# Pairs of key blocks under one VectorE pass: the positive part of a key-difference product, taken on ScalarE in front of a turn's first exponential

## The chip, the cores and the metric

One core of a Trainium2 chip runs the whole kernel. The metric is the device time of one execution in microseconds (us); the kernel before takes 1810.14 us, the median of three runs (1808.87 to 1810.49).

## What is computed

The reference is one transformer block with adaptive layer norm: attention with 16 heads of 16 dimensions over 2 sequences of 2048 tokens (32 sequence-heads in all), then a shared feed-forward network and one of eight routed experts per token. The change touches the softmax of attention:

```python
energy = jnp.einsum('nqhd,nkhd->nhqk', Q, K) / jnp.sqrt(jnp.float32(HEAD_DIM))
attn = jax.nn.softmax(energy, axis=-1)
out = jnp.einsum('nhqk,nkhd->nqhd', attn, V).reshape(N, S, EMBED)
```

The softmax subtracts each query's largest energy. The kernel finds that maximum with products of its own, one head ahead of the exponentials: it need not be exact, but it must be close, since exp overflows otherwise.

## The kernel before

**Stages.** First the projections to Q, K and V (to about 135 us, already mixed with the first head's maxima), then attention over the 32 heads (to about 1366 us), then the output projection, the shared network with the routing of tokens, and the experts. Everything is written by hand: five engine queues, semaphores, and fixed places in SBUF and PSUM. The queues are in order, so the program order of each engine is the schedule.

**Q and K as sums of bf16 parts.** `q_high` and `k_high` hold two bf16 parts of each on 64 rows, twice (rows 0 to 63 for u = 0, 64 to 127 for u = 1, which are the two halves of the queries for the maxima); `q_low` and `k_low` hold the third parts and the maxima. SyncE loads them per head from `qk_parts` in HBM (`stack`).

**Maxima of a head.** `max_product` (L1149) multiplies 128 queries by 512 keys into one PSUM bank. A head has 32 pairs m = 4t + c (query tile t of 8, key block c of 4), each with a product for u = 0 and one for u = 1: 64 products of 128x512. The products go through three banks in turn (class `Ring`); a product waits until the product three places earlier was read out. For a u = 0 product with odd m (15 of the 64) ScalarE copies the bank to `unit_sb` in `carry` (L1317), which frees the bank, and VectorE reduces the copy later (`reduce_carried`, L1277). The others VectorE reduces out of PSUM (`reduce_pair`, L1266). After a head's last pair `negate` (L1284) takes the four block maxima together, and TensorE transposes the result (`turn_maxima`, L1178).

**A turn.** Attention is a loop over heads h and 16 key tiles kt. In one turn `attend_tensor` issues, in this order:

1. `max_half`: the product (first, u = 0) of the head ahead, where first = 12 + 2(kt - 1), taken modulo 32,
2. `scores(this, 1)` (L1206): the second half of tile kt's scores, 8 matmuls of 512 columns in two row groups that run beside each other, into banks that the exponential two back must have left (`s_exp_free`),
3. `max_half`: (first, u = 1),
4. `weigh(h, kt - 1)` (L1218): probabilities times values in fp32,
5. `max_pair`: (first + 1, u = 0 and 1),
6. `scores(following, 0)`: the first half of tile kt + 1.

A turn's first exponential reads item 6 of the turn before; the second reads item 2 of its own. ScalarE's turn before the change is one `carry` (of a product in item 5 of the turn before) and the two exponentials of 128x1024 (L1338). Both exponentials must be over before `weigh` of that tile. In each head one turn also has the transposed maxima (before item 4), and one has `head_copy` on ScalarE (L1344).

**After attention.** SyncE loads expert weights (`ruT` L1499, `rdT` L1501), then the rows that GpSimd scales and scatters to the experts (`sc_x`). `rgT` was loaded by GpSimd's queue during attention, one expert every third head.

## Time and profile before

| | us |
|---|---|
| runs: median (lowest, highest) | 1810.14 (1808.87, 1810.49) |
| profiled execution: span, first to last instruction | 1807.2 |
| what lies around the span, median less span | 2.9 |
| attention, per head of 16 turns (705.31 to 744.20) | 38.89 |
| TensorE busy | 1788.2 |
| VectorE busy | 1489.3 |
| ScalarE busy | 1471.9 |
| GpSimd busy | 357.0 |

The profiled execution is known by its span; the runs' times include what lies before and after it. An engine's busy time counts from an instruction's start to its end in the record. Records of one engine overlap, since an instruction can start before the end of the one ahead of it, and the ends of matmuls are modelled. The distance from one start to the next on an engine is thus the better measure of what a step costs. The granted TensorE clock is 1.0 through attention, which is the level of 2.4 GHz.

### The profile page before, as it was taken

How to read it: one execution, taken by the hardware profiler on the slowest of the kernel's cores; microseconds unless marked ns; L12 is line 12 of the kernel's file. 1: busy time of each engine (PE TensorE's matmuls, PEld its weight loads, DVE VectorE, ACT ScalarE, POOL GpSimd, SP SyncE). 2: the span in 40 equal slices, each digit the busy share in tenths (PEclk: the TensorE clock that was granted, in tenths of full speed). 3: DMA queues.
4: the chain of work that ended last, by engine and by line, in shares of the span. 5: the costliest groups of instructions: out<-in, count | busy, mean ns of one | idle time of the engine just before them, and what ended most of it. 6: DMA issues, size and time to landing. Idle time of an engine off the chain costs nothing.

```text
span 1807.2 us, 35352 instructions
## 1 busy us (share of the span) xinstructions
PE 1788.2 (99%) x13143; PEld 809.3 (45%) x13144; DVE 1489.3 (82%) x2716; ACT 1471.9 (81%) x1908; POOL 357.0 (20%) x441
## 2 busy tenths in 40 slices
PE   9999999999999999999999999999999999999997
PEld 5533333333333333333333333333326555699996
DVE  6889999999999999999999999999935422355553
ACT  6559999999999999999999999999997411254442
POOL 6655020020000000000000200001010177233333
PEclk9999999999999999999999999999999999999998
DMA  7534131232111121111313211133124733322221
GB/s 232 151 112 120 34 89 45 82 103 60 42 45 34 43 58 59 47 34 45 91 46 98 59 42 44 42 72 86 33 69 165 286 97 117 120 81 65 67 68 42
DMA packets 87294, 145.71 MB, mean 81 GB/s; under 512 B 18692, under 2 KB 53765, under 8 KB 87020
## 3 DMA queue, kind: packets, MB, share of 16 engines
q1 hardware_dynamic: 78220, 119.22, 22.2%
q0 software_dynamic: 7936, 23.10, 4.0%
q8 instruction: 92, 1.51, 0.4%
q10 hardware_dynamic: 992, 1.44, 0.2%
q14 instruction: 54, 0.44, 0.1%
HBM read 93.85 MB, written 50.36 MB: 80 GB/s over the span
## 4 chain that ended last, share of the span: by engine, by line
PE 84%; DVE 6%; DMA 5%; ACT 2%; POOL 1%; issue 1%; SPq 1%; POOLq 0%; DVEq 0%; ACTq 0%
PE ps L1218 25%; PE ps L1206 22%; PE ps L1149 14%; PE ps L1985 8%; DVE mx L1266 4%; PE ps L2008 4%; PE ps L727 3%; DMA sc_x<-n_rows 2%; DMA sorted_in<-sc_x,slot 2%; PE ps L1551 2%; PE ps L746 1%; ACT prob L1338 1%; PE ps L1521 1%; DVE mx L1277 1%; PE ps L1858 1%
## 5 line engine op out<-in xcount | busy, mean ns | idle before, releaser
L1266 DVE TENSOR_REDUCE mx<-ps 128x1 f32<-128x512 f32 x1588 | 1004.6, 684 | 11.6 <-PE ps L1149 7.4
L1338 ACT ACTIVATE prob<-ps 128x1024 f32<-128x1024 f32 x1024 | 992.8, 1021 | 3.3 <-issue 1.6
L1149 PE MATMUL ps<-k_high,q_high 64*128 64x512 bf16 x2048 | 577.5, 382 | 0.9 <-DVE mx L1266 0.2
L1218 PE MATMUL ps<-prob,vs 128*32 128x512 f32 x4096 | 545.5, 605 | 0.2 <-ACT head_out_sb L1344 0.2
L1206 PE MATMUL ps<-q_low,k_low 34*128 34x512 bf16 x2048 | 490.6, 377 | 0.0
L1206 PE MATMUL ps<-q_high,k_high 64*128 64x512 bf16 x2048 | 490.0, 376 | 0.5 <-ACT prob L1338 0.3
L1149 PEld LDWEIGHTS ps<-k_high,q_high 64*128 64x128 bf16 x2048 | 143.2, 93 | 547.1 <-DVE mx L1266 444.3
L1277 DVE TENSOR_REDUCE mx<-unit_sb 128x1 f32<-128x512 f32 x460 | 310.8, 676 | 0.0
L1317 ACT COPY unit_sb<-ps 128x512 f32<-128x512 f32 x460 | 269.6, 586 | 5.5 <-PE ps L1149 2.0
L1206 PEld LDWEIGHTS ps<-q_low,k_low 34*128 34x128 bf16 x2048 | 143.2, 94 | 118.7
L1367 POOL CAST mb<-turned_sb 16x128 bf16<-16x128 f32 x32 | 9.0, 283 | 826.4 <-ACT turned_sb L1324 814.9
L1206 PEld LDWEIGHTS ps<-q_high,k_high 64*128 64x128 bf16 x2048 | 143.6, 95 | 53.9 <-ACT prob L1338 18.9
L1218 PEld LDWEIGHTS ps<-prob,vs 128*32 128x32 f32 x4096 | 80.6, 108 | 129.5 <-issue 118.8
L1880 ACT ACTIVATE sgate<-ps 128x512 f32<-128x512 f32 x32 | 19.1, 597 | 118.3 <-PE ps L1521 118.3
L2068 DVE TENSOR_TENSOR ehT<-esig,ps 128x512 f32<-128x512 f32 x39 | 26.8, 688 | 99.4 <-PE ps L1985 99.4
L2034 ACT ACTIVATE esig<-ps 128x512 f32<-128x512 f32 x39 | 23.3, 597 | 100.6 <-PE ps L1985 100.6
L1724 DVE TENSOR_TENSOR hid<-sgate,ps 128x512 f32<-128x512 f32 x32 | 22.0, 688 | 72.2 <-ACT sgate L1880 71.8
L1985 PE MATMUL ps<-xsT,gate_w 128*128 128x128 f32 x624 | 76.6, 276 | 0.1
L1985 PEld LDWEIGHTS ps<-xsT,gate_w 128*128 128x128 f32 x624 | 74.6, 192 | 4.4 <-DVE xsT L2061 2.5
L1985 PE MATMUL ps<-xsT,up_w 128*128 128x128 f32 x624 | 76.0, 275 | 0.0
L2008 PE MATMUL ps<-rdT,ehT 128*128 x312 | 73.6, 379 | 0.0
L1985 PEld LDWEIGHTS ps<-xsT,up_w 128*128 128x128 f32 x624 | 72.8, 192 | 0.0
(173 smaller groups left out, 1445.3 us busy)
## 6 DMA issues: line engine op xcount, KB each, us to landing
k_high<-qk_parts SPq DMA_DIRECT2D x126, 128.0 KB, 2.7
qk_parts<-parts SPq DMA_DIRECT2D x32, 384.0 KB, 3.0
k_low<-qk_parts SPq DMA_DIRECT2D x128, 64.0 KB
q_high<-qk_parts SPq DMA_DIRECT2D x126, 64.0 KB, 2.4
head_out<-head_out_sb SPq DMA_DIRECT2D x31, 256.0 KB, 2.2
sorted_in<-zero_row POOLq DMA_DIRECT2D x13, 390.0 KB, 4.6
xs<-sorted_in SPq DMA_DIRECT2D x39, 130.0 KB
q_low<-qk_parts SPq DMA_DIRECT2D x128, 32.0 KB
```

What stands on the lines that cost most here:

```text
L727: mm = pe.matmul(ps[:, 2 + n % 2, :], wqkv[:, o // 2, k, (o % 2) * P:(o % 2 + 1) * P], hT[g % CPB][:, k, :], start=(k == 0), stop=(k == 1))
L1149: pe.matmul(ps[:, ring.bank((n, m, u)), :], q_high[p][mine, t * P:(t + 1) * P], k_high[p][mine, c * CH:(c + 1) * CH], start=True, stop=Tru ...
L1206: mm = pe.matmul(ps[:, bank + u, :], keys[mine, kt * P:(kt + 1) * P], queries[mine, i * CH:(i + 1) * CH], start=(low == 0), stop=(low == 1))
L1218: mm = pe.matmul(ps[32 * j:32 * j + 32, 7, :], vs[buf(h)][:, kt, :], prob[:, (kt + 1) % 2, j * CH:(j + 1) * CH], start=(kt == 0), stop=(kt ...
L1266: dve.tensor_reduce(mx[n % 2][:, at, c:c + 1], ps[:, ring.bank(what), :], AX.X, ALU.max).then_inc(s_ring, 1)
L1277: dve.tensor_reduce(mx[n % 2][:, m // CPB, m % CPB:m % CPB + 1], unit_sb[carried_before(n, m) % NCOPY][:], AX.X, ALU.max).then_inc(s_carri ...
L1317: act.copy(unit_sb[k % NCOPY][:], ps[:, ring.bank(what), :]).then_inc(s_turned, 1)
L1338: act.activation(prob[:, (kt + 1) % 2, :].rearrange("p (u c n) -> p u c n", u=2, c=2)[:, :, half, :], ps[:, bank:bank + 2, :], ACT.Exp).th ...
L1551: mm = pe.matmul(ps[:, OUT_BANK[g % 2] + t // 2, t % 2 * D:(t % 2 + 1) * D], o[:, k, t * P:(t + 1) * P], w[:, k, :], start=(k == 0), stop= ...
L1985: mm = pe.matmul(ps[:, bank, fc * P:(fc + 1) * P], w[u][:, c, fc * P:(fc + 1) * P], xsT[u][:, c, :], start=(c == 0), stop=(c == 1))
L2008: mm = pe.matmul(ps[:, 6 + u, 0:D], ehT[u][:, c, :], rdT[:, bass.ds(e, 1), c, :].squeeze(1), start=(c == 0), stop=(c == FC - 1))
L2068: dve.tensor_tensor(ehT[u][:].rearrange("p c n -> p (c n)"), esig[u][:].rearrange("p c n -> p (c n)"), ps[:, eup_bank(k), :], ALU.mult).th ...
```

## The change

Key blocks c = 2 and c = 3 of a query tile are joined for u = 0. For the unit with m mod 4 = 2 (`steps_of`), TensorE multiplies the queries not by block 2 but by the difference of the keys, block 2 less block 3 (`k_step`). ScalarE takes the positive part, Relu, into `step_sb` (`take_step`, in place of `carry`). For m mod 4 = 3 (`folded`) VectorE adds `step_sb` to the product of block 3 and takes the maximum of the sum in one `tensor_tensor_reduce`: max(q k2 - q k3, 0) + q k3 is the larger of the two. The column of block 2 in `mx` is set to the lowest value once. There are 8 such units per head, 245 in all (5 of head 1, 8 of each of heads 2 to 31); the 460 copies and the 460 reductions of copies are gone.

`take_step` stands inside `exps`, ahead of the first exponential of turn kt, and reads the product of item 1 of the same turn kt. It does so in the turns with even kt; in those with odd kt ScalarE has the two exponentials alone.

Beside it: GpSimd makes the key differences of each sequence in two bf16 parts (`key_steps`, 3 operations for each of 2 halves), SyncE stores them and loads them per head with two more transfers (`load_key_steps`); `wuT` and `wdT` are loaded later; the last expert's `rgT` is loaded after attention by SyncE, ahead of `ruT`.

```diff
-def carried(n, m, u):
-    return u == 0 and m % 2 == 1 and m != LEAD - 1 and (n >= 2 or n == 1 and m >= LEAD)
+def steps_of(n, m, u):
+    return u == 0 and m % CPB == STEP and (n >= 2 or n == 1 and m >= LEAD)
+def folded(n, m, u):
+    return u == 0 and m % CPB == STEP + 1 and steps_of(n, m - 1, u)
...
+        def key_steps(pool, step, half):
+            step(pool.tensor_tensor(k_from[half][:], k_from[half][:], k_to[half][:], ALU.subtract))
+            step(pool.tensor_copy(step_parts[half][:, 0, :], k_from[half][:]))
+            pool.tensor_tensor(step_parts[half][:, 1, :], k_from[half][:], step_parts[half][:, 0, :],
+                               ALU.subtract).then_inc(s_kstep, 1)
...
+        def load_key_steps(sp, h):
+            n = num(h)
+            sp.wait_ge(s_kstepst, 16 * HALF * (n // H + 1))
+            mine = slice(n * DH, (n + 1) * DH)
+            for part in range(2):
+                sp.dma_start(k_step[n % 2][part * LROWS:(part + 1) * LROWS, :],
+                             step_dram[part:part + 1].to_broadcast([2, B * D, CH])[:, mine, :]
+                             .rearrange("a d t -> d a t")).then_inc(s_kstep_in[n % 2], 16)
...
+            keys = k_high[p][mine, c * CH:(c + 1) * CH]
+            if steps_of(n, m, u):
+                pe.wait_ge(s_kstep_in[n % 2], 32 * (n // 2 + n % 2))
+                keys = k_step[n % 2][mine, :]
...
-                dve.tensor_reduce(mx[n % 2][:, at, c:c + 1], ps[:, ring.bank(what), :], AX.X,
-                                  ALU.max).then_inc(s_ring, 1)
...
+                if folded(*what):
+                    above = step_sb[steps_before(n, m - 1) % NSTEP][:]
+                    dve.wait_ge(s_turned, ring.taken((n, m - 1, u)))
+                    dve.tensor_tensor_reduce(above, bank, above, 1.0, LOWEST, ALU.add, ALU.max,
+                                             largest).then_inc(s_ring, 1)
+                else:
+                    dve.tensor_reduce(largest, bank, AX.X, ALU.max).then_inc(s_ring, 1)
...
-                    if m % 2 == 0:
-                        reduce_carried(dve, n, m - 1)
...
-            what, k = (who, first + 1, 0), carried_before(who, first + 1)
...
-            act.wait_ge(s_max, ring.made(what))
-            wait(act, s_carried, k - NCOPY + 1)
-            act.copy(unit_sb[k % NCOPY][:], ps[:, ring.bank(what), :]).then_inc(s_turned, 1)
+            what = (who, first, 0)
...
+            act.wait_ge(s_max, ring.made(what))
+            if k >= NSTEP:
+                act.wait_ge(s_ring, step_folded[k - NSTEP])
+            act.activation(step_sb[k % NSTEP][:], ps[:, ring.bank(what), :], ACT.Relu).then_inc(s_turned, 1)
...
                 for half in range(2):
+                    if not half and n + kt:
+                        take_step(act, n, kt)
...
-                    carry(act, KT * n + kt)
                     exps(n, kt)
...
+            sp.dma_start(rgT[:, E - 1:E], io["rgT"][:, E - 1:E]).then_inc(s_expert_late, 16)
             for e in range(E):
                 sp.dma_start(ruT[:, e:e + 1], io["ruT"][:, e:e + 1]).then_inc(s_expert_late, 16)
```

On ScalarE, in attention, before the change (`unit_sb` is a copy of a product, `prob` an exponential):

```order
L1338 ACTIVATE prob<-ps 128x2x512 [waits s_score]
L1317 COPY unit_sb_85<-ps 128x512 [waits s_carried,s_max]
L1338 ACTIVATE prob<-ps 128x2x512 [waits s_score,s_prob_free]
L1338 ACTIVATE prob<-ps 128x2x512 [waits s_score]
L1317 COPY unit_sb_84<-ps 128x512 [waits s_carried,s_max]
L1338 ACTIVATE prob<-ps 128x2x512 [waits s_score,s_prob_free]
```

The same place with the change (`step_sb` is the positive part):

```order
L1384 ACTIVATE step_sb_84<-ps 128x512 [waits s_ring,s_max,s_prob_free]
L1409 ACTIVATE prob<-ps 128x2x512 [waits s_score] x2
L1409 ACTIVATE prob<-ps 128x2x512 [waits s_score,s_prob_free]
L1409 ACTIVATE prob<-ps 128x2x512 [waits s_score]
L1384 ACTIVATE step_sb_85<-ps 128x512 [waits s_ring,s_max,s_prob_free]
```

There is now one read of a product in two turns instead of in each. On TensorE the order is that of before; with the change a turn with even kt reads (L1223 is the products of maxima, L1280 the scores, L1292 `weigh`):

```order
L1280 MATMUL ps<-q_high_94,k_high_70 128x512 [waits s_exp_free]
L1280 MATMUL ps<-q_high_94,k_high_70 128x512
L1280 MATMUL ps<-q_low_97,k_low_71 128x512 x2
L1223 MATMUL ps<-k_step_109,q_high_92 128x512 [waits s_kstep_in0,s_ring]
L1280 MATMUL ps<-q_high_94,k_high_70 128x512 [waits s_exp_free]
L1280 MATMUL ps<-q_high_94,k_high_70 128x512
L1280 MATMUL ps<-q_low_97,k_low_71 128x512 x2
L1223 MATMUL ps<-k_high_68,q_high_92 128x512 [waits s_ring]
L1292 MATMUL ps<-prob,vs_67 32x512 [waits s_exp_free]
```

The product of the difference (fourth row) stands behind the scores that the turn's first exponential reads, and that exponential now stands behind the product's reader. On VectorE, before and after around the end of a head (`mneg` is the head's negated maxima):

```order
L1266 TENSOR_REDUCE mx_80<-ps 128x1 [waits s_max] x3
L1277 TENSOR_REDUCE mx_80<-unit_sb_84 128x1 [waits s_turned]
L1266 TENSOR_REDUCE mx_80<-ps 128x1 [waits s_max] x3
L1277 TENSOR_REDUCE mx_80<-unit_sb_85 128x1 [waits s_turned]
```

```order
L1346 TENSOR_REDUCE mx_80<-ps 128x1 [waits s_max]
L1346 TENSOR_REDUCE mx_81<-ps 128x1 [waits s_max] x4
L1351 TENSOR_REDUCE mneg<-mx_80 128x16 [waits s_ring]
L1346 TENSOR_REDUCE mx_81<-ps 128x1 [waits s_max]
L1343 ISA step_sb_85,mx_81<-ps,step_sb_85 128x512 [waits s_turned,s_max]
L1343 ISA mx_81 128x1
L1346 TENSOR_REDUCE mx_81<-ps 128x1 [waits s_max] x6
```

Of eight products in two turns VectorE now reads six alone and two together; the joined pass is two rows, the pass and the write of its result.

## Rows read from the trace of the kernel before

**Rows 1.** The page: busy time by engine.

```profile
PE 1788.2 (99%) x13143; PEld 809.3 (45%) x13144; DVE 1489.3 (82%) x2716; ACT 1471.9 (81%) x1908; POOL 357.0 (20%) x441
```

**Rows 2.** Chain that ended last, 640 to 760 us, by line.

```profile
by line: PE ps L1218 40.6%; PE ps L1206 36.1%; PE ps L1149 22.9%; PE ps L1178 0.5%
```

**Rows 3.** Timeline, one steady turn: start us, us, engine line op, names, shapes, count.

```profile
712.53 0.39 PE L1149 MATMUL ps<-k_high,q_high 64*128 64x512 bf16 x2
...
712.95 0.59 ACT L1317 COPY unit_sb<-ps 128x512 f32<-128x512 f32 x1
...
713.00 1.90 DVE L1266 TENSOR_REDUCE mx<-ps 128x1 f32<-128x512 f32 x3
...
713.19 0.38 PE L1149 MATMUL ps<-k_high,q_high 64*128 64x512 bf16 x1
...
713.46 1.94 ACT L1338 ACTIVATE prob<-ps 128x1024 f32<-128x1024 f32 x2
...
713.94 1.07 PE L1218 MATMUL ps<-prob,vs 128*32 128x512 f32 x8
...
714.94 0.39 PE L1149 MATMUL ps<-k_high,q_high 64*128 64x512 bf16 x2
```

**Rows 4.** Timeline, TensorE in the last head, which has no maxima beside it.

```profile
1340.11 1.07 PE L1218 MATMUL ps<-prob,vs 128*32 128x512 f32 x8
1341.11 0.39 PE L1206 MATMUL ps<-q_high,k_high 64*128 64x512 bf16 x2
...
1342.08 0.64 PE L1218 MATMUL ps<-prob,vs 128*32 128x512 f32 x4
```

**Rows 5.** The page: groups that the change touches (busy, mean ns; idle before, releaser).

```profile
L1266 DVE TENSOR_REDUCE mx<-ps 128x1 f32<-128x512 f32 x1588 | 1004.6, 684 | 11.6 <-PE ps L1149 7.4
...
L1149 PEld LDWEIGHTS ps<-k_high,q_high 64*128 64x128 bf16 x2048 | 143.2, 93 | 547.1 <-DVE mx L1266 444.3
L1277 DVE TENSOR_REDUCE mx<-unit_sb 128x1 f32<-128x512 f32 x460 | 310.8, 676 | 0.0
```

**Rows 6.** Timeline, ScalarE: a copy out of PSUM and the exponential behind it.

```profile
1337.45 0.59 ACT L1344 COPY head_out_sb<-ps 128x512 f32<-128x512 f32 x1
1337.91 3.87 ACT L1338 ACTIVATE prob<-ps 128x1024 f32<-128x1024 f32 x4
```

**Rows 7.** Timeline, last head, where TensorE waits for an exponential.

```profile
1329.41 3.91 ACT L1338 ACTIVATE prob<-ps 128x1024 f32<-128x1024 f32 x4 [0.41 <-PE ps L1206]
...
1331.40 0.10 PEld L1206 LDWEIGHTS ps<-q_high,k_high 64*128 64x128 bf16 x2 [0.61 <-ACT prob L1338]
...
1331.94 0.16 PEld L1218 LDWEIGHTS ps<-prob,vs 128*32 128x32 f32 x8 [0.43 <-issue]
```

**Rows 8.** Timeline, the turn with the transposed maxima (L1178).

```profile
702.69 0.39 PE L1149 MATMUL ps<-k_high,q_high 64*128 64x512 bf16 x2
...
703.76 0.21 DVE L1284 TENSOR_REDUCE mneg<-mx 128x16 f32<-128x64 f32 x1
...
704.11 0.27 PE L1178 MATMUL ps<-ident,mneg 128*16 128x128 f32 x1
...
705.31 0.39 PE L1149 MATMUL ps<-k_high,q_high 64*128 64x512 bf16 x2
```

**Rows 9.** Timeline, TensorE: the pair that ends the turn of rows 3's last line.

```profile
717.46 0.39 PE L1149 MATMUL ps<-k_high,q_high 64*128 64x512 bf16 x2
```

**Rows 10.** Groups on VectorE, 1560 to 1807 us.

```profile
L2068 DVE TENSOR_TENSOR ehT<-esig,ps 128x512 f32<-128x512 f32 x39 | 26.8, 688 | 99.4 <-PE ps L1985 99.4
...
L2082 DVE CAST cix<-xs 128x1 uint32<-128x1 f32 x39 | 5.7, 147 | 0.0
```

**Rows 11.** Chain that ended last, 1412 to 1540 us, in order of time.

```profile
1422.23 15.13 DMA sc_x<-n_rows
```

**Rows 12.** Timeline, SyncE: the first eight of sixteen expert loads.

```profile
1412.73 3.85 SPq L1499 DMA_DIRECT2D ruT<-in_ruT  x8
```

**Rows 13.** Groups by line, 60 to 200 us.

```profile
L919 POOL TENSOR_TENSOR rest<-qf,parts 128x512 f32<-128x512 f32 x17 | 19.7, 1157 | 28.6 <-ACT parts L824 28.6
```

More of the change, by code:

```diff
@@ L69 @@
 SLOTS = 6
-NCOPY = 2
+NSTEP = 2
+STEP = 2
+LOWEST = -3.0e38
 BESIDE = LEAD
@@ L90, in wait, with steps_before @@
         eng.wait_ge(semaphore, n)
[L93 to L102 removed]
+def steps_of(n, m, u):
+    return u == 0 and m % CPB == STEP and (n >= 2 or n == 1 and m >= LEAD)
+def folded(n, m, u):
+    return u == 0 and m % CPB == STEP + 1 and steps_of(n, m - 1, u)
+def steps_before(n, m):
+    return sum(steps_of(k, j, 0) for k in range(n + 1) for j in range(PAIRS if k < n else m))
 class Region:
@@ L210, in block_kernel @@
         wgT = held("wgT", [P, HALF, F])
+        late_weights_at = held.at
         wuT = held("wuT", [P, HALF, F])
@@ L397, in block_kernel @@
         s_turned = sem("s_turned")
-        s_carried = sem("s_carried")
+        s_kstep = sem("s_kstep")
+        s_kstepst = sem("s_kstepst")
+        s_kstep_in = [sem(f"s_kstep_in{i}") for i in range(2)]
         s_mb = sem("s_mb")
@@ L562, in unit, with kept, full @@
             return 2 * g + o // 2 if g < CPB and o % 2 == 0 else EARLY + 2 * g + o // 2 if g < CPB else UQ * g + o
+        def kept(g, o):
+            return o >= 2 and g % CPB in (STEP, STEP + 1)
+        def full(g, o):
+            return (k_from, k_to)[g % CPB - STEP][o - 2] if kept(g, o) else qf[unit(g, o) % UQ]
+        UNITS_AT = {unit(g, o): (g, o) for g in range(NCH) for o in range(UQ)}
         def adapt(pe, first):
@@ L695, in project_sync @@
                 sp.dma_start(dst[:], src).then_inc(s_late, 16)
+            for half in range(HALF):
+                store_key_steps(sp, 0, half)
             store(CPB + 1, 2, 3)
@@ L818, in take @@
                 n = unit(g, o)
-                slot, bank, scale = n % UQ, 2 + n % 2, 0.25 if o < 2 else 1.0
+                bank, scale = 2 + n % 2, 0.25 if o < 2 else 1.0
                 act.wait_ge(s_unit, n + 1)
                 act.wait_ge(s_qf_free, n + 1)
-                act.activation(qf[slot][:], ps[:, bank, :], ACT.Identity, bias=bqk[:, o:o + 1], scale=scale)
+                if kept(g, o) and g >= CPB:
+                    act.wait_ge(s_kstepst, 16 * HALF)
+                act.activation(full(g, o)[:], ps[:, bank, :], ACT.Identity, bias=bqk[:, o:o + 1], scale=scale)
                 act.wait_ge(s_parts[n % SLOTS], 16 * (n // SLOTS + 1))
@@ L918, in remainder @@
                 pool.wait_ge(s_qbank_free, AHEAD + n + 1)
-                pool.tensor_tensor(rest[n % UQ][:], qf[n % UQ][:], parts[n % SLOTS][:, 0, :],
+                pool.tensor_tensor(rest[n % UQ][:], full(*UNITS_AT[n])[:], parts[n % SLOTS][:, 0, :],
                                    ALU.subtract).then_inc(s_rest, 1)
@@ L1077, in prepare @@
                         sp.dma_start(xg_dram[c], xg[c][:]).then_inc(s_xgst, 16)
+                if n == XB_AT + 4:
+                    for half in range(HALF):
+                        store_key_steps(sp, 1, half)
+                if n == XB_AT + 5:
+                    sp.wait_ge(s_kstepst, 16 * HALF * B)
+                    for dst, name in ((wuT, "wuT"), (wdT, "wdT")):
+                        sp.dma_start(dst[:], io[name]).then_inc(s_shared, 16)
                 if n == XB_AT + 1:
@@ L1309, in carry @@
                 first, who = first - PAIRS, n + 2
-            if g < 2 or who >= NH:
+            if kt == 0:
+                first, who = LEAD + 2 * (KT - 1) - PAIRS, n + 1
+            what = (who, first, 0)
+            if who >= NH or not steps_of(*what):
                 return
-            what, k = (who, first + 1, 0), carried_before(who, first + 1)
-            if not carried(*what):
-                return
+            k = steps_before(who, first)
             act.wait_ge(s_max, ring.made(what))
-            wait(act, s_carried, k - NCOPY + 1)
-            act.copy(unit_sb[k % NCOPY][:], ps[:, ring.bank(what), :]).then_inc(s_turned, 1)
+            if k >= NSTEP:
+                act.wait_ge(s_ring, step_folded[k - NSTEP])
+            act.activation(step_sb[k % NSTEP][:], ps[:, ring.bank(what), :], ACT.Relu).then_inc(s_turned, 1)
+        step_folded = [ring.taken((n, m + 1, 0)) for n in range(NH) for m in range(PAIRS) if steps_of(n, m, 0)]
         def take_turned(act, n):
@@ L1427, in attend_gpsimd @@
                     bias(1, 0)
+                    for half in range(HALF):
+                        key_steps(pool, step, half)
                 if n == FIRST_AT + 6:
```

67 lines of the change are left out of this document (36 added, 31 removed).

## The prediction

> **What bounds the kernel now.** I began with the page's busy shares. TensorE is busy 99% of the span [rows 1], but the ends of matmuls are modelled, so that alone proves nothing; VectorE, ScalarE and TensorE all look full in attention. The chain of waits for a stretch of attention settles it: all of it lies on TensorE, none on VectorE or ScalarE [rows 2]. Then the timeline of one steady turn [rows 3]. I measure from the pair of products that ends a turn, and call its start P = 0 (712.53). The product of item 1 of the next turn starts at 0.66, `weigh` at 1.41, the next pair at 2.41. A head is sixteen such turns.
>
> Does TensorE wait for VectorE at the end of that turn? The page puts 444.3 us of the idle time of its weight loads down to VectorE [rows 5], and that is the number on which a gain would rest. But from `weigh` to the next matmul it is 1.00 us with products of maxima behind it [rows 3], and 1.00 us in the last head, where VectorE has none left [rows 4]. So the 1.00 us is TensorE's own. The last head's turn is 1.97 [rows 4]; two more passes of 512 columns (the pair, and the two halves beside the scores, 0.22 each: the first product stands at 0.66 behind the pair and two such steps of scores) make 2.41. **TensorE is the bound, with nothing to spare, and the change takes no matmul from it.** VectorE does four products in 2.41 us and keeps up: 0.61 from start to start (1.90 less 0.68, halved) [rows 3].
>
> ScalarE has a little slack. Its two exponentials start 0.92 apart (1.94 less the 1.02 of one [rows 3]) and end at 715.40, which is 2.87; the scores that may not overwrite them start 0.66 behind the next pair, at 3.07. TensorE starts 0.05 after an exponential's end: in rows 7 the second exponential starts at 1330.33 (0.92 after the first), ends at 1331.35, and the weight load comes at 1331.40. So the slack is 3.07 - 2.87 - 0.05 = 0.15 us.
>
> **VectorE's part.** 460 reductions of copies go (310.8 us busy [rows 5]) and 245 products are no longer reduced alone, while 245 of the remaining passes become joined ones. The trace has no joined pass. Its nearest row is a 128x512 fp32 operation on an SBUF and a PSUM operand, 688 ns; the write of the result is nearest to the 128x1 operation, 147 ns [rows 10]. Start to start I take 0.70, bounds 0.61 (as a reduction) and 1.38 (the streaming of 512 elements, 688 - 147 = 541 ns, twice, and 0.15 each for overhead and write). Seven passes in two turns take 6 x 0.61 + 0.70 = 4.36 of 4.81 us. As TensorE is the bound, this gains nothing; cost 0.
>
> The Trainium skill speaks against the joined pass: "Vector Engine (DVE) Microarchitecture Reference", section "Points that are easy to get wrong", says that the scalar-tensor-tensor shape with two SBUF sources that are not bf16 runs at half throughput, since no port is left for the accumulator. Here one source is in PSUM, so by its words the rule does not bite; the trace has no accumulating operation to show it. If it did, the upper bound above would hold, and the third rival.
>
> **ScalarE's part, on which the sum rests.** Before, each turn's copy reads the pair at P: the pair ends at 0.39, the copy starts at 0.42, the first exponential at 0.93 [rows 3]. Now in a turn with even kt the positive part reads the product that starts at 0.66. That ends 0.38 later and is read 0.03 after that, so at 1.07. From the start of such a read to the exponential behind it is 0.46 where only ScalarE decides [rows 6]; I take 0.47. The exponentials then start at 1.54 and 2.46 (+0.92), the second ends at 3.48 (+1.02), and TensorE's next second-half scores can start at 3.53 (+0.05) instead of 3.07. **The exponentials came 0.61 later, 0.15 was slack, and 0.46 is lost on the engine that is the bound.** Behind these scores nothing is made up: scores to `weigh` is 0.54 alone [rows 7] plus 0.22 for the other half-product, 0.76 against the 0.75 of before (1.41 - 0.66), and 1.00 follows. So the pair after next stands at 3.53 + 0.76 + 1.00 = 5.29 instead of 4.81. From this lap 0.48, from the slack 0.46: I take **0.47 us per two turns.** The turn with odd kt cannot win it back: ScalarE has only 1.84 us of work there and stands idle, but the next positive part must wait for 5.29 + 1.07 anyhow. That is a closed loop: product, positive part, two exponentials, scores, `weigh`, pair, scores, product.
>
> How many: 245 units, of which 185 in plain turns (31 each for kt 2, 4, 6, 8, 10, 30 for kt 14), 30 at kt 12 and 30 at kt 16.
>
> - 185 x 0.47 = 87.0 us.
> - kt 12 has the transposed maxima. Before, `mneg` starts at 1.07 after one reduction, the transposition at 1.42, the next pair at 2.62 [rows 8]; with the odd turn 5.03. Now the pair's first product is not copied any more but reduced first, so `mneg` starts 0.60 later and ends at 1.88, the transposition comes at 1.93 (+0.05), 0.51 later, the next pair at 3.13. The scores after it start at 3.79, beyond 3.53, so that the loop adds nothing: 30 x 0.51 = 15.3 us.
> - kt 16: before, 2.52 (714.94 to 717.46 [rows 3, 9]) and 2.41, together 4.93; now 5.29. 30 x 0.36 = 10.8 us.
>
> Sum in attention 113.1 us.
>
> **The rest.** GpSimd's six operations on key blocks, 1.16 us each by their nearest row [rows 13], are 7 us beside a queue that idled 28.6 us in that stretch, and its results are wanted a unit later: 0, upper bound 3. If that cover were gone, ScalarE's casts would be late first. The second sequence's six, and two more loads per head on SyncE, run an entire head or more ahead of their reader: 0. `rgT` of the last expert is a seventeenth load of 512 KB ahead of `sc_x`, whose landing, 15.13 us [rows 11], waits for the sixteen and starts the chain of the scatters. They took from 1412.73 [rows 12] to 1437.36, 1.5 us each: +1.5, bounds 0 and 3.
>
> Total: +114.6. The profiled span of 1807.2 becomes 1921.8; with the 2.9 us around a span that the median has, 1924.7, as the median plus 114.6 is: **1925 us**.
>
> **The rivals.** (1) *VectorE is what bounds, and the change frees it.* For: the 444.3 us [rows 5], and VectorE's unbroken row of passes. Then two turns need 4.36 instead of 4.81, 245 x 0.45 = 110 us less: 1700 us; it decides if the positive part is not waited for and the 1.00 us shrinks. Against: the same 1.00 in the last head. If only part of this holds, it is faster by less. Chance 0.05. (2) *The product is read in time after all*, since ScalarE's exponentials have slack that I don't see; then TensorE keeps 2.41, and only kt 12 costs: between 1811 and 1827 us. Against: the order of the three queues leaves no way round it. Chance 0.04, half of it within 0.2%. (3) *The joined pass is slow* (1.38). Then VectorE, from the pair at 2.41: pass at 2.83, next 4.21, the odd turn's first product 4.82 to 5.50, and the pair after next, whose bank it holds, not before 5.55 instead of 5.29: 245 x 0.26 = 64 us more, 1989 us. It decides from a joined pass of 1.12 on. Chance 0.08. (4) *The loop holds, but loses less*, as the matmuls' modelled ends put the product's real end earlier, or the held back scores let later matmuls pack better: 0.25 to 0.4 per two turns, with kt 12 and kt 16 and the 1.5 us some 1878 to 1910. Chance 0.13. The forecast itself, 0.44 to 0.52 per two turns and the other bounds, has 0.70.
>
> **How the numbers follow.** The forecast's own range is 1916 to 1940 (185 x 0.03 below, 245 x 0.05 above, and the two small bounds). To leave out no more than 2 in 10, I reach down into the fourth case, to 1893, and up to 1945, which leaves out the third. What a measurement of this kernel can tell from no change is about 0.2%, 3.6 us. Slower by more: 0.70 + 0.13 + 0.08 and half of the second, 0.93; within it 0.02; faster 0.05.
>
> **What would show it.** Right: in turns with even kt the positive part starts about 0.03 after the end of the product beside the scores, at 1.07 behind the pair; TensorE's second-half scores of the odd turn wait for an exponential; pairs stand 2.41 and 2.88 apart in turn; ScalarE is idle before the positive part by about 1.0 us; VectorE idles in each turn; a head takes 42.5 us instead of 38.89. Wrong: pairs 2.41 apart or less throughout, no idle time of ScalarE before its read, or, for the third rival, waits of the pair for VectorE and a joined pass of over 1 us.

## The result, and the profile after

The kernel with the change takes 1942.07 us, the median of four runs (1941.20 to 1942.73), against 1810.27 beside it: **7.3% slower, ratio 1.0728 (95% interval 1.0713 to 1.0743)**. The forecast was 1925 us with a range of 1893 to 1945. The sign, the engine and the mechanism held; 132 us were lost where 114.6 were worked out. That is 2 us beyond the forecast's own bounds (1916 to 1940), and inside the stated range by 3.

The profiled execution has a span of 1939.4 us and a time of 1941.20. All of the loss is in attention: from the first to the last `weigh` it is 1366.0 us instead of 1234.2 (+131.8), the part ahead of it changed by -1.2 us (132.3 for 133.6), the part behind it by +1.7 (441.1 for 439.4).

The page, busy time by engine and the chain that ended last, by engine (the first line answers to [rows 1]):

```profile
PE 1890.8 (97%) x13143; PEld 769.3 (40%) x13144; DVE 1382.1 (71%) x2719; ACT 1352.9 (70%) x1693; POOL 367.9 (19%) x452
...
PE 56%; ACT 28%; issue 11%; DVE 4%; DMA 0%; POOLq 0%; DVEq 0%; POOL 0%; ACTq 0%
```

VectorE and ScalarE each work over 100 us less than before and the kernel is slower. TensorE is still "97% busy", although it now waits in every second turn: for a bound, this share says little. The chain does, here for 640 to 760 us (it answers to [rows 2], which held nothing but TensorE):

```profile
by line: ACT prob L1409 30.9%; PE ps L1292 21.2%; issue 16.6%; PE ps L1280 12.2%; ACT step_sb L1384 9.5%; PE ps L1223 7.0%; DVE mx L1346 2.1%; PE ps L1252 0.5%; DVE mneg L1351 0.2%
```

One lap of two turns of it, start, length and what:

```profile
743.26 1.04 PE ps L1292 x8
744.30 1.01 issue
745.32 0.60 ACT step_sb L1384
745.91 1.84 ACT prob L1409 x2
747.75 0.05 issue
747.80 0.61 PE ps L1280 x4
748.40 0.22 PE ps L1223
748.62 1.04 PE ps L1292 x8
```

That is the forecast's closed loop: 748.62 - 743.26 = 5.36 us. (The four matmuls of L1280 are one half of a tile's scores, two with `q_high` and two with `q_low`; item 2 of a turn has four, not eight.) The 1.01 us of "issue" are the pair, the scores and the difference product between `weigh` and the positive part, which the chain couldn't tie to it. The timeline shows them (start us, us, engine line op, names, shapes, count; it answers to [rows 3]):

```profile
744.19 0.39 PE L1223 MATMUL ps<-k_high,q_high 64*128 64x512 bf16 x2
...
744.85 0.38 PE L1223 MATMUL ps<-k_step,q_high 64*128 64x512 bf16 x1
...
745.32 0.60 ACT L1384 ACTIVATE step_sb<-ps 128x512 f32<-128x512 f32 x1 [1.10 <-issue]
745.36 0.09 PEld L1223 LDWEIGHTS ps<-k_high,q_high 64*128 64x128 bf16 x1 [0.19 <-DVE mx L1346]
...
745.81 3.77 ACT L1409 ACTIVATE prob<-ps 128x1024 f32<-128x1024 f32 x4
...
746.68 0.39 PE L1223 MATMUL ps<-k_high,q_high 64*128 64x512 bf16 x2
...
747.10 0.69 DVE L1343 CUSTOM_DVE_ANT_0 step_sb<-ps,step_sb 128x512 f32<-128x512 f32 x1 [0.60 <-PE ps L1223]
...
747.72 0.08 DVE L1343 DVE_READ_ACCUMULATOR2_ANT mx<- 128x1 f32 x1
747.72 1.88 DVE L1346 TENSOR_REDUCE mx<-ps 128x1 f32<-128x512 f32 x3
747.79 0.10 PEld L1280 LDWEIGHTS ps<-q_high,k_high 64*128 64x128 bf16 x2 [0.58 <-ACT prob L1409]
...
748.55 0.16 PEld L1292 LDWEIGHTS ps<-prob,vs 128*32 128x32 f32 x8 [0.43 <-issue]
```

ScalarE sits idle for 1.10 us, reads the product that it had to wait for, and its second exponential ends late enough to hold TensorE's scores for 0.58. The pair comes at 744.19 and 746.68, 2.49 apart; the next one 2.87 behind that (2.87 or 2.88 in all plain laps). VectorE idles 0.60 in front of the joined pass. TensorE's one wait for it in these rows, the 0.19 at 745.36, lies inside the lap and costs nothing here. The groups of the page say the same over the program (busy, mean ns; idle before, releaser; the second and third lines answer to the first two of [rows 5], whose third has no counterpart):

```profile
L1384 ACT ACTIVATE step_sb<-ps 128x512 f32<-128x512 f32 x245 | 146.5, 598 | 244.2 <-issue 242.1
...
L1346 DVE TENSOR_REDUCE mx<-ps 128x1 f32<-128x512 f32 x1558 | 982.2, 684 | 88.0 <-PE ps L1223 84.3
L1223 PEld LDWEIGHTS ps<-k_high,q_high 64*128 64x128 bf16 x1803 | 120.6, 93 | 551.1 <-DVE mx L1346 483.3
L1343 DVE CUSTOM_DVE_ANT_0 step_sb<-ps,step_sb 128x512 f32<-128x512 f32 x245 | 169.5, 692 | 164.0 <-PE ps L1223 164.0
```

The idle time of weight loads put down to VectorE, 444.3 us before, is 483.3 now, with VectorE visibly idle. So this figure doesn't tell what a faster VectorE would give back.

### The profile page after: what moved, and what is told of

The parts are those of the page before. It is cut to its first block, busy times and chain, and to the rows that moved or that the text cites. A ratio compares the mean times of both kernels' runs of the same rounds, so it can differ in the third digit from the quotient of the medians.

```text
span 1939.4 us, 35464 instructions
## 1 busy us (share of the span) xinstructions
PE 1890.8 (97%) x13143; PEld 769.3 (40%) x13144; DVE 1382.1 (71%) x2719; ACT 1352.9 (70%) x1693; POOL 367.9 (19%) x452
## 3 DMA queue, kind: packets, MB, share of 16 engines
q8 instruction: 94, 1.54, 0.3%
## 4 chain that ended last, share of the span: by engine, by line
PE 56%; ACT 28%; issue 11%; DVE 4%; DMA 0%; POOLq 0%; DVEq 0%; POOL 0%; ACTq 0%
ACT prob L1409 21%; PE ps L1292 16%; PE ps L1280 9%; PE ps L2058 8%; ACT step_sb L1384 6%; PE ps L1223 6%; PE ps L1594 5%; PE ps L1931 3%; PE ps L2081 3%; PE ps L759 3%; DVE mx L1346 2%; PE ps L778 1%; PE ps L1624 1%; PE ps L1252 0%; PE ps L611 0%
## 5 line engine op out<-in xcount | busy, mean ns | idle before, releaser
L1346 DVE TENSOR_REDUCE mx<-ps 128x1 f32<-128x512 f32 x1558 | 982.2, 684 | 88.0 <-PE ps L1223 84.3
L1409 ACT ACTIVATE prob<-ps 128x1024 f32<-128x1024 f32 x1024 | 973.9, 1034 | 15.6 <-PE ps L1280 14.4
L1292 PE MATMUL ps<-prob,vs 128*32 128x512 f32 x4096 | 545.5, 605 | 0.2 <-ACT head_out_sb L1415 0.2
L1223 PE MATMUL ps<-k_high,q_high 64*128 64x512 bf16 x1803 | 487.5, 384 | 0.8 <-DVE mx L1346 0.2
L1280 PE MATMUL ps<-q_high,k_high 64*128 64x512 bf16 x2048 | 448.5, 378 | 18.5 <-ACT prob L1409 0.6
L1280 PE MATMUL ps<-q_low,k_low 34*128 34x512 bf16 x2048 | 447.0, 377 | 0.0
L1223 PEld LDWEIGHTS ps<-k_high,q_high 64*128 64x128 bf16 x1803 | 120.6, 93 | 551.1 <-DVE mx L1346 483.3
L1384 ACT ACTIVATE step_sb<-ps 128x512 f32<-128x512 f32 x245 | 146.5, 598 | 244.2 <-issue 242.1
L1343 DVE CUSTOM_DVE_ANT_0 step_sb<-ps,step_sb 128x512 f32<-128x512 f32 x245 | 169.5, 692 | 164.0 <-PE ps L1223 164.0
L1280 PEld LDWEIGHTS ps<-q_high,k_high 64*128 64x128 bf16 x2048 | 124.7, 94 | 196.9 <-ACT prob L1409 142.2
L1280 PEld LDWEIGHTS ps<-q_low,k_low 34*128 34x128 bf16 x2048 | 124.6, 94 | 68.1
L1292 PEld LDWEIGHTS ps<-prob,vs 128*32 128x32 f32 x4096 | 80.6, 107 | 160.6 <-issue 149.5
L1223 PE MATMUL ps<-k_step,q_high 64*128 64x512 bf16 x245 | 92.2, 376 | 0.0
```

The lines of the kernel that those rows point to most:

```text
L1223: pe.matmul(ps[:, ring.bank((n, m, u)), :], q_high[p][mine, t * P:(t + 1) * P], keys, start=True, stop=True).then_inc(s_max, 1)
L1280: mm = pe.matmul(ps[:, bank + u, :], keys[mine, kt * P:(kt + 1) * P], queries[mine, i * CH:(i + 1) * CH], start=(low == 0), stop=(low == 1))
L1292: mm = pe.matmul(ps[32 * j:32 * j + 32, 7, :], vs[buf(h)][:, kt, :], prob[:, (kt + 1) % 2, j * CH:(j + 1) * CH], start=(kt == 0), stop=(kt ...
L1343: dve.tensor_tensor_reduce(above, bank, above, 1.0, LOWEST, ALU.add, ALU.max, largest).then_inc(s_ring, 1)
L1346: dve.tensor_reduce(largest, bank, AX.X, ALU.max).then_inc(s_ring, 1)
L1384: act.activation(step_sb[k % NSTEP][:], ps[:, ring.bank(what), :], ACT.Relu).then_inc(s_turned, 1)
```

## The experiments

Theories: **the lap** (product, ScalarE's read, exponentials, scores, `weigh`, pair), in which the place of ScalarE's read sets the price; against it **the new work** (joined pass, difference keys), and **VectorE as the bound**. Each time is a median beside runs of the kernel before on the same chip; ratios are to that kernel. Its median differs from chip to chip (1806.65 to 1810.65 us), so versions are compared by their ratios. "Turns" are the distances from one `weigh` to the next in the profiled execution.

### The place of the read

**Only the place.** No joined pass, the difference keys are made and loaded but not multiplied, block 2 does not enter the maxima, and the same read stands at the same place:

```diff
-                keys = k_step[n % 2][mine, :]
+                pass
...
-                    dve.tensor_tensor_reduce(above, bank, above, 1.0, LOWEST, ALU.add, ALU.max,
-                                             largest).then_inc(s_ring, 1)
+                    dve.tensor_reduce(largest, bank, AX.X, ALU.max).then_inc(s_ring, 1)
...
-            act.activation(step_sb[k % NSTEP][:], ps[:, ring.bank(what), :], ACT.Relu).then_inc(s_turned, 1)
+            act.activation(step_sb[k % NSTEP][:], ps[:, ring.bank(what), :], ACT.Identity).then_inc(s_turned, 1)
```

> Leaves out: the key difference (the product is the ordinary one of block 2), the joined pass (VectorE reduces block 3 alone) and the maxima of block 2. ScalarE's read stays at the place of the positive part, as an identity. Everything that the change adds except that read's place is gone, and VectorE has the same seven passes in two turns. Theory (the lap product, ScalarE's read, exponentials, scores): 1942 +-8 us, pairs 2.49 and 2.88 apart. Rival (the joined pass or the difference keys carry part of the price): clearly lower, towards 1810-1900 us.

Measured: 1937.13 us, ratio 1.0723 (1.0705 to 1.0741), turns 2.49 and 2.88. The change's own ratio is 1.0728. The whole loss is there without the joined pass and without the difference product. What this version shares with the change is the place of the read, one read in two turns instead of two, seven passes of VectorE, and the new work of GpSimd and SyncE. The last two don't cost, as the version with both reads early, below, has them too and runs in the time of before; the missing second read is priced there as well.

**A shorter read there.** On top of the last one; three quarters of the product's columns are not read:

```diff
-            act.activation(step_sb[k % NSTEP][:], ps[:, ring.bank(what), :], ACT.Identity).then_inc(s_turned, 1)
+            act.activation(step_sb[k % NSTEP][:, 0:128], ps[:, ring.bank(what), 0:128], ACT.Identity).then_inc(s_turned, 1)
```

> As read_place_only, and the read covers 128 of its 512 columns. By the trace a 128-column copy takes 0.24 us and a 512-column one 0.58, so the lap gets 0.34 us shorter in the plain turns and at kt 16 (215 times 0.34 = 73 us), and nothing at kt 12. Theory: 1869 us, between 1860 and 1885. Rival (it is the wait for the product, not the read's length behind it, that sets the price, with ScalarE catching up): 1935-1942 us.

Measured: 1868.94 us, ratio 1.0348 (1.0331 to 1.0365), turns 2.49 and mostly 2.55 or 2.56: 68 us less than with the full read, where 73 were expected. The pair, the read and the exponential in one lap:

```profile
763.73 0.39 PE L1223 MATMUL ps<-k_high,q_high 64*128 64x512 bf16 x2
...
764.85 0.28 ACT L1383 ACTIVATE step_sb<-ps 128x128 f32<-128x128 f32 x1 [0.81 <-issue]
...
765.03 1.94 ACT L1408 ACTIVATE prob<-ps 128x1024 f32<-128x1024 f32 x2
...
767.01 0.10 PEld L1280 LDWEIGHTS ps<-q_high,k_high 64*128 64x128 bf16 x2 [0.26 <-ACT prob L1408]
```

The read starts 1.12 behind the pair, as before, for it waits for the same product. The exponential follows 0.18 later instead of 0.49, and the held scores come 3.28 behind the pair instead of 3.60. Those 0.32 us, 215 times, are 69 us. What ScalarE does between product and exponential is paid by the kernel to the full.

**Read in front of the second exponential:**

```diff
-                    if not half and n + kt:
+                    if half and n + kt:
```

> The changed kernel with the positive part in front of the turn's second exponential instead of the first; nothing else moves. Theory of the lap (the read of the product waits beside the scores and pushes both exponentials, which gate TensorE's next scores): the first exponential is back at 0.93 us behind the pair, the positive part follows at 1.84 without waiting, the second exponential ends at about 3.35 instead of 3.56, so each two turns lose about 0.33 instead of 0.55 us: 1885 to 1897 us. Rival (what costs is the joined pass or the work itself, not where the read stands): 1942 us as now.

Measured: 1897.8 us, ratio 1.0492 (1.0475 to 1.0510), turns 2.49 and 2.68; 0.8 us above the expected range, and far from the rival's 1942. The first exponential fills part of the wait for the product, as expected; the second one is still behind the read, and TensorE's scores wait 0.30 us for it (at 745.04 in that trace).

**The product earlier.** Blocks 1 and 2 are paired, so that the difference product is in the pair that ends a turn, and ScalarE reads it where the kernel before made its copy:

```diff
-STEP = 2
+STEP = 1
...
+            g = KT * n + kt
+            if g < 2:
+                return
+            n, kt = (g - 2) // KT, (g - 2) % KT + 1
...
-            if kt == 0:
-                first, who = LEAD + 2 * (KT - 1) - PAIRS, n + 1
-            what = (who, first, 0)
+            what = (who, first + 1, 0)
```

> The whole change, but for key blocks 1 and 2 in place of 2 and 3: the difference product is then one of the pair that ends a turn, and ScalarE reads it where the copy of before stood, in front of a turn's first exponential but a whole group of scores earlier. Theory of the lap: the exponentials are back at their place and the 0.55 us per two turns are gone; what stays is 0.08 us in each turn behind a pair whose first product VectorE reads itself (seen as turns of 2.49 instead of 2.41 in the changed kernel): 1822 to 1832 us. Rival (VectorE was the bound, so one pass fewer in eight gives time back): clearly under 1810 us. Rival (joined pass costs): over 1850 us.

Measured: 1831.92 us, ratio 1.0130 (1.0113 to 1.0147), turns 2.44 and 2.49. With all of the new work still in it (the key differences are stored a little earlier), 108 of the 132 us are gone by the ratios. Of what is left, 24 us or 0.11 in two turns, 0.08 is a wait in the turn that doesn't begin with the difference product:

```profile
746.82 0.09 PEld L1223 LDWEIGHTS ps<-k_high,q_high 64*128 64x128 bf16 x1 [0.19 <-DVE mx L1346]
```

The second half product wants the bank of the pair's first product. Before, ScalarE copied that one out at once, and now it is VectorE's first of two. In the other turn the read starts 0.47 behind its pair (748.61 for a pair at 748.14) and not 0.42 as before the change, so the bank comes free later; that turn is 2.44 instead of 2.41. There the read carries the wait for `prob` and not the one for the product, of which more under the order of the waits below.

**The product in front of the scores of item 6:**

```diff
+                    ahead = (who, first + 2) if first + 2 < PAIRS else (plus(who, 1), 0)
+                    if kt < KT and after >= (1 if ahead[0] == plus(h, 1) else 2) and steps_of(num(ahead[0]), ahead[1], 0):
+                        max_half(pe, *ahead, 0)
```

> The changed kernel with one move on TensorE: the difference product of a turn is issued in front of the scores that the turn's first exponential reads, instead of behind them. ScalarE keeps its order. Theory of the lap: the product starts 0.22 us behind the pair instead of 0.66, the positive part at 0.70 instead of 1.13, the gated scores at about 3.18 instead of 3.61, near their free place at 3.07; what is left is about 0.12 us per two turns and the turn with the transposed maxima: 1835 to 1860 us. Rival (the positive part in front of the first exponential costs wherever its product stands): above 1920 us.

Measured: 1903.14 us, ratio 1.0512 (1.0495 to 1.0530), turns 2.65 and 2.52: a miss, below the rival's 1920 as well. The product didn't follow the pair:

```profile
747.10 0.39 PE L1223 MATMUL ps<-k_high,q_high 64*128 64x512 bf16 x2
747.55 0.09 PEld L1223 LDWEIGHTS ps<-k_step,q_high 64*128 64x128 bf16 x1 [0.36 <-DVE mx L1349]
747.56 0.39 PE L1223 MATMUL ps<-k_step,q_high 64*128 64x512 bf16 x1
```

It starts 0.46 behind the pair, not 0.22, because its bank in the ring of three is released by VectorE only then (0.45 to 0.48 in 241 of the 245); and all scores of item 6 now stand behind it. A product can't be moved forward without its bank.

### The size of the lap

**The two waits of the positive part, in the other order:**

```diff
-            act.wait_ge(s_max, ring.made(what))
             if k >= NSTEP:
                 act.wait_ge(s_ring, step_folded[k - NSTEP])
+            act.wait_ge(s_max, ring.made(what))
```

> The changed kernel with the two waits in front of the positive part in the other order, so that the wait for the product comes last. In the changed kernel the positive part starts 0.086 us behind the product's recorded end, the copy of before 0.033 us; between them lies a separate wait instruction of ScalarE that ends 0.045 us before the positive part starts. If that instruction is the reason, 245 laps get 0.05 us shorter: about 1930 us. Rival (the product beside the scores really ends later than its record says, as matmul ends are modelled): no change, 1942 us.

Measured: 1946.83 us, ratio 1.0763 (1.0745 to 1.0781), turns 2.49 and 2.91. It goes the wrong way, by a little: 0.03 a lap, which the heads of the profiles show too (43.44 us for 43.21). So the order matters, but the wait that the read carries itself isn't the one written last.

**The wait for the product as the first of all,** ahead of the wait for `prob`:

```diff
             def exps(n, kt):
+                if n + kt:
+                    take_step(act, n, kt)
                 act.wait_ge(s_prob_free, KT * n + kt + 1)
```

> The changed kernel with the wait for the product moved ahead of the wait for prob, so that it is the first wait of the positive part in program order. In the changed kernel ScalarE holds the wait for the product in a separate instruction, which ends 0.045 us before the positive part starts; putting that wait last made it 0.118 us instead of 0.086. If an instruction carries its first wait itself, the positive part now starts about 0.035 us behind the product's end, as the copy of before did, and each lap is 0.05 us shorter: 1927 to 1932 us. Rival (a product beside scores really ends later than recorded): 1942 us, unchanged.

Measured: 1930.27 us, ratio 1.0657 (1.0639 to 1.0675), turns 2.49 and 2.83. Product and read of the three, the change's in the timeline above (product 744.85, read 745.32), then the wait last, then first:

```profile
742.81 0.38 PE L1223 MATMUL ps<-k_step,q_high 64*128 64x512 bf16 x1
...
743.31 0.60 ACT L1384 ACTIVATE step_sb<-ps 128x512 f32<-128x512 f32 x1 [0.64 <-DVE mx L1346]
```

```profile
745.97 0.38 PE L1223 MATMUL ps<-k_step,q_high 64*128 64x512 bf16 x1
...
746.38 0.60 ACT L1384 ACTIVATE step_sb<-ps 128x512 f32<-128x512 f32 x1 [1.04 <-PE ps L1223]
```

From the product's end to the read it is 0.09 us with the change, 0.12 with the wait behind the other one, 0.03 with it in front (0.47, 0.50 and 0.41 start to start, less 0.38; over all 245 reads the records give medians of 0.086, 0.118 and 0.036). Only in the last does the profile name the product as the releaser. The waiting instructions of ScalarE's queue show more (count; duration in ns, least/median/most; first and last start). With the change:

```profile
L1383 ACTq EVENT_SEMAPHORE  x243: 2050/2177/2179, 143.0 to 1450.8; - x122
```

With the wait for the product behind the other one, at the read of 743.31:

```profile
L1383 ACTq EVENT_SEMAPHORE  x1: 38/38/38, 743.2 to 743.2; - x1
```

With the wait for the product first:

```profile
L1383 ACTq EVENT_SEMAPHORE  x243: 17/17/17, 144.1 to 1440.7; - x122
```

The semaphores in the records tell which is which. In all three versions the read carries the wait that the program issues first, and one separate instruction ahead of it has the rest. With the change the read carries the wait for `prob`, and the separate instruction waits 2.18 us for the product; the read follows 0.045 behind its end. With the two exchanged the same instruction has both, and its record of 38 ns starts only behind the product's end. With the product's wait first the read carries it, and the separate instruction, for the ring, has nothing to wait for. By the ratios this is 13 of the 132 us (1.0728 to 1.0657), and so most of the 17 that the forecast was low.

### Is VectorE's saved pass worth anything?

**The copy instead of the joined pass.** Block 2's product is an ordinary one, copied at the place of the positive part, and VectorE reduces the copy in a pass of its own, between two products of the next turn (eight passes in two turns again). In the second version it does so one product later:

```diff
+                    if u and m % CPB == 0:
+                        copied(*((n, m - 2) if m else (n - 1, PAIRS - 2)))
                     dve.tensor_reduce(largest, bank, AX.X, ALU.max).then_inc(s_ring, 1)
```

> The changed kernel without key differences and without the joined pass: TensorE multiplies by block 2 as before the change, ScalarE copies that product at the place of the positive part, VectorE reduces the copy and the product of block 3 in two passes. Only the place of ScalarE's read is left of the change in attention. Theory of the lap: 1942 us, within 8. Rival (the joined pass or the product of differences costs): much nearer to 1810 us.

> As plain_copy (no key differences, no joined pass, only the place of ScalarE's read is left of the change), but VectorE reduces the copy one product later, behind the second product of the next turn. In plain_copy that reduction stood ahead of one whose bank TensorE's next early product needs, and TensorE waited for VectorE (0.25 us at 745.44), so the lap was 5.47 instead of 5.37. Theory of the lap: with that out of the way 1942 us, within 8, with the same 2.49 and 2.88 from turn to turn. Rival (the difference or the joined pass has a price of its own): well under 1942, towards 1810 us.

Measured: 1979.68 us, ratio 1.0944 (1.0925 to 1.0962), turns 2.67 and 2.80; the later one 1984.63 us, ratio 1.0955 (1.0937 to 1.0973), turns 2.98 and 2.49. Both miss, by about 40 us. They were meant to isolate the read's place, but put a VectorE pass into the way of a bank. They also let `negate` wait for the pass over the copy: the turn with the transposed maxima is mostly 3.37 us in the first and 3.81 in the second, for 3.18 with the change, which in 30 heads is 6 and 19 us of the 40. The chain of the later one, one lap:

```profile
747.70 0.39 PE ps L1223
748.08 0.99 PE ps L1292 x8
749.08 0.37 PE ps L1223 x2
749.45 0.68 DVE mx L1349
750.13 1.79 DVE mx L1351 x3
751.92 0.59 DVE mx L1335
752.51 0.61 DVE mx L1351
753.12 0.05 issue
753.17 0.39 PE ps L1223
```

Here VectorE is in the lap, with L1335 the pass over the copy. So in the new layout, where only every second turn has an early release of a bank, a pass more costs about 40 us, and the joined pass saves it; it saves it from a layout that costs more. Only the first experiment above separates the read's place.

**Both reads early.** The version with the early difference product, and ScalarE copies the same product of the other turns too, as before; VectorE reduces those copies. Seven passes in two turns, an early release in each turn, each read ahead of the wait for `prob`:

```diff
-def steps_of(n, m, u):
+def read_out(n, m, u):
...
+            if steps_of(*what):
+                act.activation(step_sb[k % NSTEP][:], ps[:, ring.bank(what), :], ACT.Relu).then_inc(s_turned, 1)
+            else:
+                act.copy(step_sb[k % NSTEP][:], ps[:, ring.bank(what), :]).then_inc(s_turned, 1)
```

> The whole change with key blocks 1 and 2, as early_product, and with two things of the kernel before kept: ScalarE also copies the first product of each other pair (VectorE reduces the copy), and its read stands ahead of the wait for prob. VectorE has seven passes for eight products as in the change. Theory (TensorE's 2.41 us a turn bounds, VectorE's saved pass is worth nothing): turns of 2.41 throughout, 1808 to 1813 us, the same as before. Rival (VectorE was the bound before the change): clearly faster than before, 1700 to 1790 us.

Measured: 1807.64 us, the median of ten runs (1806.71 to 1808.99), ratio 0.9985 (0.9975 to 0.9994), turns of 2.41 as before the change, with the same two longer ones in a head (2.62, and 2.49 for 2.52). Here VectorE's saved pass is what is left of the change, with all of the new work of GpSimd and SyncE, and it brings at most a quarter of one per cent. **TensorE's 2.41 us stay although VectorE is spared one pass in eight.** It is the best complete version that was run. Against the version with the earlier product it has two things more, the early release in each turn and the order of the waits, and they were not tried one by one.

**TensorE relieved,** in the kernel before and in the version with both reads early. In 14 of 16 turns the value products leave out three quarters of their columns, and with them that part of the output:

```diff
+                w = CH if kt in (0, KT - 1) else 128
...
-                    mm = pe.matmul(ps[32 * j:32 * j + 32, 7, :], vs[buf(h)][:, kt, :],
-                                   prob[:, (kt + 1) % 2, j * CH:(j + 1) * CH], start=(kt == 0), stop=(kt == KT - 1))
+                    mm = pe.matmul(ps[32 * j:32 * j + 32, 7, 0:w], vs[buf(h)][:, kt, :],
+                                   prob[:, (kt + 1) % 2, j * CH:j * CH + w], start=(kt == 0), stop=(kt == KT - 1))
```

> The kernel before, but the value products of kt 1 to 14 cover 128 of 512 columns, which leaves that part of the output out and takes up to 0.7 us of TensorE's 1.00 us out of these turns. Theory (TensorE and VectorE are both nearly full in the turn, VectorE by four starts 0.61 apart = 2.44): almost nothing is gained, 1790-1810 us. Rival (TensorE alone is the bound, VectorE has room): over 60 us less, under 1750 us.

> The version with both reads early (both_reads: seven VectorE passes in two turns and one copy or positive part in each turn), with the same cut of the value products. Theory (the pass that the change saves on VectorE is worth something once TensorE is relieved, up to ScalarE's own bound of 0.51 + 0.92 + 0.92 = 2.35 us a turn): 1770-1795 us, below before_less_tensor. Rival (ScalarE already bounds both, or VectorE's saved pass is worth nothing here either): equal to before_less_tensor within 5 us.

Measured: 1790.78 us, ratio 0.9917 (0.9901 to 0.9934), and 1763.62 us, ratio 0.9768 (0.9749 to 0.9788), the second 6 us under its range. The 1763.62 are the median of three executions (1763.42 to 1765.53); a fourth took 5093.75 us, and no run shows why. The cut takes 0.57 us from a `weigh` (from 1.00 to 0.43), some 255 us over the 448 of them, and the kernel before gives back 16. What holds it then, in its chain:

```profile
715.55 0.59 DVE mx L1278
716.15 1.79 DVE mx L1267 x3
717.94 0.59 DVE mx L1278
718.53 1.79 DVE mx L1267 x3
720.33 0.59 DVE mx L1278
```

VectorE, pass behind pass: 0.60 each, 64 a head, 38.2 us of the head's 38.5. (Most turns are 2.32; the one with the transposed maxima is mostly 3.14.) So before the change VectorE's passes filled all but 0.6 us of a head's 38.8. The saved pass is worth 27 us once TensorE has room, and next to nothing as long as it hasn't. It is not worth more, though 245 passes of 0.60 are 147 us: in the relieved version ScalarE is busy for 996 of the 1000 us from 200 to 1200, and TensorE and VectorE for 957 and 942.

## Why the prediction came out as it did

- **TensorE is the bound, VectorE's saved pass is worth 0: right.** Both reads early keeps 2.41 us a turn and 1807.64 us. The prediction's reason, 1.00 us from `weigh` to the next pair with and without maxima [rows 3, 4], held. What it had too simple is "keeps up": VectorE was the next bound, less than 2% away, as the relieved kernels show.
- **The joined pass: right, and rather cheaper.** It lasts 692 ns, and 0.62 us from its start (747.10) to the next pass (747.72), with the reading of the accumulator; 0.70 was taken, 1.38 the upper bound. The half throughput that the Trainium skill gives for two SBUF sources ("Vector Engine (DVE) Microarchitecture Reference", "Points that are easy to get wrong") doesn't show with one source in PSUM; whether this instruction, which the trace calls a custom one, has the form that the page speaks of is not shown. The third rival is out.
- **The lap: right in kind, too small in size; this is the term that was off.** The prediction put the read 0.03 behind the product's end, at 1.07, and the exponential 0.47 behind that, at 1.54. Measured are 1.13 (745.32 - 744.19) and 1.62 (745.81), so the scores come at 3.61 (747.80 - 744.19) instead of 3.53, and the lap is 5.36 instead of 5.29: 0.55 lost on the 4.81 of before instead of 0.47. The 0.03 was read from a copy that carries its wait for the product itself, since that is the first one issued. Here the wait for `prob` is issued first, and the read started 0.09 after the product; with the product's wait in front it was 0.03, and the kernel 12 us faster. The other part, 0.49 from read to exponential for 0.47, is a reading of a neighbouring row to two hundredths.
- **Count and sum.** 185 times 0.55 is 102 us instead of 87.0. kt 16 lost 0.43 (5.36 less 4.93) instead of 0.36, 13 us instead of 10.8.
- **kt 12: right in kind.** The first product of the pair is reduced first, `mneg` and the transposed maxima come later, and the turn took 3.18 us instead of 3.13. The odd turn behind it was put at its old 2.41 and took 2.50; together 5.68 instead of 5.54, 0.65 lost instead of 0.51, 19 us instead of 15.3.
- **These terms give 134 us, attention lost 132.** An undisturbed head is 43.21 instead of 38.83 us, 4.38 more, and by these terms it should be 4.38. In the profiled execution of before, though, 11 of 30 heads are longer than that, by up to 0.66 us and 2.8 us together, and with the change three are 0.28 longer; that is most of the difference.
- **Odd turns of 2.49: not foreseen.** The forecast had 2.41 and 2.88. The extra 0.08 is the half product that waits 0.19 for VectorE, since nothing is copied out of the pair any more. The lap covers it, so it costs nothing here, but it is most of the 24 us that the version with the earlier product still loses.
- **The rest: no cost from GpSimd and SyncE, right; behind attention, right by luck.** Their new work does not show. The part behind attention is 1.7 us longer where 1.5 was forecast for the seventeenth load, but not for that reason. GpSimd's first work on `sc_x` did start 1.4 us later behind the last `weigh` (71.1 for 69.7), but the last scatter started 1.5 earlier (181.1 for 182.6) and the matmuls of the routed experts 0.7 earlier (210.3 for 211.0); the time was lost after that. The version with only the place of the read, with the same seventeenth load, takes 437.3 us there instead of 441.1, and before it was 439.4: a term of 1.5 us can't be told in these profiles.
- **The rivals.** The product wasn't read in time (second), and the lap did not lose less (fourth) but more. With 0.55 it lies outside the 0.44 to 0.52 to which the forecast gave 0.70, on the side for which there was no case. That the stated range still holds the result is in part luck: its upper end was moved from the forecast's own 1940 to 1945, which takes in none of its cases.

With the lap, kt 12 and kt 16 as measured, the same working gives 1810.1 + 134 + 1.5 = 1946 us, 4 over the result.

## What to carry to other kernels

Moving a read costs what stands behind it on its queue, not what it takes: a 0.6 us read of a product that is 0.66 us younger cost 0.55 us in every second turn, because two exponentials and the scores that reuse their banks stood behind it, and it saved a pass of an engine that nobody waited for. Before pairing or merging work, place the pairs so that the value read is the oldest one there is, and give back each early release of a bank that the merging takes away. When an instruction has several waits, try issuing the one that comes last in time first (in this program the instruction itself carried the wait issued first), and look whether the profile names it as the releaser.

## What the runs showed of the hardware that was not expected

- The order of the waits in front of one ScalarE instruction moved its start by up to 0.08 us: 0.036, 0.086 and 0.118 us behind the end of the product, as the instruction carried that wait itself, or a separate one carried it last or first of two. Once in a lap of 5.36 us the step from 0.086 to 0.036 is 12 us in 1942. The copies of before and those of the version with both reads early, which carry the wait for the product too, start 0.033 behind it.
- A VectorE pass that adds a PSUM and an SBUF operand of 128x512 fp32 and takes the maximum costs 692 ns, and 0.62 us start to start, as much as a plain reduction (684 ns).
- With the same 13143 matmuls TensorE's busy time rose from 1788.2 to 1890.8 us, though their records are no longer than before (378 and 379 ns for one of maxima or scores). The wait hides beside the record of a running matmul: in each lap the scores start 1.12 instead of 0.66 behind their pair (747.80 and 746.68), and since the product of 747.34 is shown for 0.38 us, only 0.08 of those 0.46 count as idle.
